# Every fourth key block weighed in f32, GpSimd without subtractions and sums, ScalarE's steps placed later: attention with a routed feed-forward layer on one core

## The reference

```python
xn = _layernorm(x)
# attention, 8 heads of 64, one key and one value head for all of them
xa = layer_norm(xn, norm_g)
q, (k, v) = xa @ Wq, split(xa @ Wkv)
q, k = l2norm(q * 16) * 4, l2norm(k) * 4
attn = softmax(einsum('bhid,bjd->bhij', q, k))          # 2048 x 2048 for each head
s = layer_norm(einsum('bhij,bjd->bhid', attn, v) @ Wout, out_norm_g)
# routed feed-forward layer: 8 experts, top 2, capacity 2560 rows each
wy = (gelu(xg @ w1 + b1) @ w2 + b2) * gating
g = silu(segment_sum(wy))
return x + s * g
```

## Time and profile before

| | |
|---|---|
| median of 3 runs | 3028.18 us |
| the profiled execution's own time | 3029.31 us |
| its span, first to last instruction | 3027.6 us |
| busy: PE, DVE, ACT, POOL | 2777.8, 2012.2, 1910.8, 1125.2 us |
| mean granted TensorE clock | 0.974 |

### The profile page before, as it was taken

One profiled execution on the slowest core, in us unless ns is written; L12 is line 12 of the kernel. 1 busy time (PEld: TensorE's weight loads), 2 busy tenths in 40 slices (PEclk: granted clock), 3 DMA queues, 4 the chain that ended last, 5 costly groups with the idle time before them and its releaser, 6 DMA issues.

```text
span 3027.6 us, 86214 instructions
## 1 busy us (share of the span) xinstructions
PE 2777.8 (92%) x38213; PEld 1847.3 (61%) x38277; DVE 2012.2 (66%) x2798; ACT 1910.8 (63%) x2435; POOL 1125.2 (37%) x707
## 2 busy tenths in 40 slices
PE   4999999988999989999999999999888889888896
PEld 3566666655666657666666666655555555555564
DVE  5777787789888733333333343378788888888775
ACT  6777767756766655565656565466666666666664
POOL 2444444414787400000000000055566656566454
PEclk8999999999999989999999999999999999999997
DMA  2213222003332011221121221101111111111101
GB/s 98 93 66 109 89 76 92 28 32 99 126 120 85 6 55 50 79 72 65 63 86 59 68 74 51 38 24 32 49 47 42 49 42 40 42 43 44 30 23 45
DMA packets 111013, 184.12 MB, mean 61 GB/s; under 512 B 12648, under 2 KB 78128, under 8 KB 110640
## 3 DMA queue, kind: packets, MB, share of 16 engines
q1 hardware_dynamic: 98352, 145.04, 14.6%
q0 software_dynamic: 12288, 33.57, 3.5%
HBM read 92.58 MB, written 85.98 MB: 59 GB/s over the span
## 4 chain that ended last, share of the span: by engine, by line
PE 64%; DVE 17%; ACT 9%; issue 7%; POOL 2%; DMA 1%; SPq 0%; ACTq 0%; DVEq 0%; POOLq 0%
PE pair L607 15%; PE bank L687 14%; PE pair L673 14%; DVE arena L1194 9%; ACT arena L843 6%; PE bank L637 5%; PE bank L628 4%; PE bank L626 4%; PE bank L588 2%; PE bank L546 2%; DVE o_rest L1129 1%; PE bank L657 1%; DVE q_n L1115 1%; POOL routed_rows L1271 1%; PE bank L576 1%
## 5 line engine op out<-in xcount | busy, mean ns | idle before, releaser
L1194 DVE TENSOR_TENSOR arena<-arena 128x1024 bf16<-128x1024 f32 (+1 forms) x817 | 1091.9, 1347 | 351.6 <-ACT arena L843 349.0
L843 ACT ACTIVATE arena<-pair 128x1024 f32<-128x1024 f32 (+1 forms) x1032 | 1017.2, 1015 | 319.4 <-PE pair L607 309.7
L607 PE MATMUL pair<-qT,kT 128*128 128x512 f16 (+1 forms) x4096 | 903.0, 388 | 136.7 <-ACT arena L843 133.6
L626 PE MATMUL bank<-vhl,arena 128*128 128x65 bf16 x8192 | 654.4, 194 | 4.0 <-DVE att L1187 4.0
L1313 POOL TENSOR_TENSOR arena<-arena 128x1024 bf16<-128x1024 f32 (+1 forms) x215 | 440.6, 2049 | 578.6 <-ACT arena L843 561.3
L628 PE MATMUL bank<-vhl,arena 128*128 128x64 bf16 x8192 | 655.0, 195 | 0.0
L626 PEld LDWEIGHTS bank<-vhl,arena 128*128 128x128 bf16 x8192 | 573.6, 100 | 56.3 <-DVE att L1187 4.4
L628 PEld LDWEIGHTS bank<-vhl,arena 128*128 128x128 bf16 x8192 | 555.3, 98 | 52.3 <-issue 1.9
L607 PEld LDWEIGHTS pair<-qT,kT 128*128 128x128 f16 (+1 forms) x4096 | 205.5, 96 | 598.8 <-issue 405.0
L1243 POOL TENSOR_TENSOR q_small<-q_small,minus_half 128x8 f32<-128x8 f32 x64 | 142.8, 2231 | 1015.8 <-DVE q_small L1111 1014.8
L637 PE MATMUL bank<-vhl,arena 128*128 128x65 bf16 x8192 | 421.2, 194 | 22.9 <-DVE arena L1194 17.1
(11 more groups left out here) (191 smaller groups left out, 2448.6 us busy)
## 6 DMA issues: line engine op xcount, KB each, us to landing
routed_rows<-h_f SPq DMA_DIRECT2D x80, 256.0 KB, 4.5
att<-routed_rows SPq DMA_DIRECT2D x40, 512.0 KB, 4.3
expert_rows<-att SPq DMA_DIRECT2D x40, 512.0 KB, 2.9
raw<-in_L_ffn_w SPq DMA_DIRECT2D x32, 512.0 KB
xn_rows<-s_hl SPq DMA_DIRECT2D x16, 512.0 KB, 2.9
xT_out<-xn_rows SPq DMA_DIRECT2D x64, 128.0 KB
w_lo<-in_L_attn_x SPq DMA_DIRECT2D x64, 128.0 KB
out<-w_lo SPq DMA_DIRECT2D x64, 128.0 KB, 2.0
```

The costliest lines, as they stand in the source:

```text
L607: t = nc.tensor.matmul(into, kT[g // BG % 2][rows, part, keys], qT[g % 2][rows, h, :], start=(turn == 0), stop=(turn == 1))
L626: nc.tensor.matmul(bank[:, at:at + DH + 1], p_top[:, s, cols, 1], V[:, kb, 0:DH + 1], start=(kb == 0 and qb == 0), stop=False, skip_group_ ...
L843: nc.scalar.activation(p_f32[:, n % NP, columns(n)], pairs[n % 2][:, columns(n)], ACT.Exp).then_inc(exped, 1)
L1194: nc.vector.tensor_tensor(p_lo[:, n % NP, c], p_f32[:, n % NP, c], p_top[:, n % NP, c, 1], ALU.subtract).then_inc(lowed, 1)
```

## The change

In steps with `n % 4 == 3` the key block is weighed with the f32 exponentials as stationary operand and a copy of the values in f32 (`v_f32`, with its column of ones) as moving operand: one matmul of 65 columns for each head and block of 128 queries in place of three. Such a step has no low weights. In the built program each f32 matmul is two weight loads and two matmuls. `low` is left on DVE alone, for three steps of four, in the scatter stretch too. The sum with x in `combine` goes from POOL to DVE. For later tiles some side steps are placed later by one or two slots.

```diff
-    on_pool = [n % 4 == 3 and not R_AT <= place["scores", n] < SCATTER_AT + 2 * NT for n in range(NSTEP)]
+    in_f32 = [n % GT == GT - 1 for n in range(NSTEP)]
+    low_to = np.cumsum([not wide for wide in in_f32]).tolist()
...
+        v_f32 = [sb(f"v_f32{i}", [P, BG, DH + 1], F32) for i in range(2)]
...
+                    if in_f32[n]:
+                        for qb in range(GT):
+                            cols = slice(i * BANK + qb * P, i * BANK + (qb + 1) * P)
+                            t = nc.tensor.matmul(bank[:, qb * (DH + 1):(qb + 1) * (DH + 1)], p_f32[:, s, cols],
+                                                 v_f32[b % 2][:, kb // GT, :], start=False, stop=(kb == KB - 1),
+                                                 skip_group_check=True)
+                        continue
...
-                pe.wait_ge(lowed, n + 1 - pool_to[n])
-                pe.wait_ge(lowed_pool, pool_to[n])
-                for i, g, h, kb in halves(n):
+                pe.wait_ge(lowed, low_to[n])
+                for i, g, h, kb in () if in_f32[n] else halves(n):
...
-                yield from clock.at(Q_AT[t_id] + 6)
+                yield from clock.at(Q_AT[t_id] + (6 if t_id < GT else 7))
...
-                yield from clock.at(C_AT[t_id] + 10)
+                yield from clock.at(C_AT[t_id] + 12)
                 act.wait_ge(f_both, i + 1)
...
+                nc.vector.memset(v_f32[b % 2][:, gi, DH:DH + 1], 1.0)
+                nc.vector.tensor_copy(v_f32[b % 2][:, gi, 0:DH], v_f[:, GT - 1, :])
...
-                yield from clock.at(Q_AT[t_id] + 7)
+                yield from clock.at(Q_AT[t_id] + (7 if t_id < GT else 9))
                 dve.wait_ge(q_hi, t_id + 1)
...
-                yield from clock.at(C_AT[t_id] + 9)
+                yield from clock.at(C_AT[t_id] + 10)
                 dve.wait_ge(f_first, i + 1)
...
-                yield from clock.at(C_AT[t_id] + 12)
+                yield from clock.at(C_AT[t_id] + 14)
                 dve.wait_ge(c_tanh, i + 1)
...
+                dve.wait_ge(c_times, i + 1)
+                dve.wait_ge(x_again_loaded[i % 2], 16 * (i // 2 + 1))
+                dve.wait_ge(out_stored[i % 2], 16 * (i // 2))
+                nc.vector.tensor_tensor(res[i % 2], w, x_again[i % 2], ALU.add).then_inc(c_added, 1)
...
-                    if a is not None and not on_pool[a]:
+                    if a is not None and not in_f32[a]:
                         low(a)
...
-                yield from clock.at(C_AT[t_id] + 14)
-                pool.wait_ge(c_times, i + 1)
-                pool.wait_ge(x_again_loaded[i % 2], 16 * (i // 2 + 1))
-                pool.wait_ge(out_stored[i % 2], 16 * (i // 2))
-                nc.gpsimd.tensor_tensor(res[i % 2], c_work[i % 2][:, D:2 * D], x_again[i % 2],
-                                        ALU.add).then_inc(c_added, 1)
-
-            def low(n):
-                pool.wait_ge(exped, n + 1)
-                pool.wait_ge(weighed, n - NP + 1)
-                c = columns(n)
-                nc.gpsimd.tensor_tensor(p_lo[:, n % NP, c], p_f32[:, n % NP, c], p_top[:, n % NP, c, 1],
-                                        ALU.subtract).then_inc(lowed_pool, 1)
...
-                yield from clock.at(C_AT[t_id] + 15)
+                yield from clock.at(C_AT[t_id] + 16)
                 sp.wait_ge(c_added, i + 1)
```

More of the change, by code:

```diff
@@ L199, in columns @@
         return slice(active[0] * BANK, (active[-1] + 1) * BANK)
-    on_pool = [n % 4 == 3 and not R_AT <= place["scores", n] < SCATTER_AT + 2 * NT for n in range(NSTEP)]
-    pool_to = np.cumsum(on_pool).tolist()
+    in_f32 = [n % GT == GT - 1 for n in range(NSTEP)]
+    low_to = np.cumsum([not wide for wide in in_f32]).tolist()
+    assert CUT % GT == 0 and BEHIND % GT == 0
     def last_step(hh):
@@ L361, in build_program @@
                              "q_hi", "q_lo", "q_turned", "qT_copied")]
-        scored, exped, lowed, lowed_pool, weighed = [sem(n) for n in (
-            "scored", "exped", "lowed", "lowed_pool", "weighed")]
+        scored, exped, lowed, weighed = [sem(n) for n in ("scored", "exped", "lowed", "weighed")]
         head_inv, divided = sem("head_inv"), sem("divided")
@@ L1301, in combine @@
                         bass.IndirectOffsetOnAxis(gather_from[k][:, t_id:t_id + 1], 0)).then_inc(y_gathered[i % 2], 16)
-                yield from clock.at(C_AT[t_id] + 14)
-                pool.wait_ge(c_times, i + 1)
-                pool.wait_ge(x_again_loaded[i % 2], 16 * (i // 2 + 1))
-                pool.wait_ge(out_stored[i % 2], 16 * (i // 2))
-                nc.gpsimd.tensor_tensor(res[i % 2], c_work[i % 2][:, D:2 * D], x_again[i % 2],
-                                        ALU.add).then_inc(c_added, 1)
-            def low(n):
-                pool.wait_ge(exped, n + 1)
-                pool.wait_ge(weighed, n - NP + 1)
-                c = columns(n)
-                nc.gpsimd.tensor_tensor(p_lo[:, n % NP, c], p_f32[:, n % NP, c], p_top[:, n % NP, c, 1],
-                                        ALU.subtract).then_inc(lowed_pool, 1)
             def main(kind, a, b):
-                if kind == "att" and a is not None and on_pool[a]:
-                    low(a)
+                pass
             clock.run(slots, main, [constants()] + [statistics(g) for g in reversed(range(NG))] + [route()] + [
```

## The result

The changed kernel takes 3064.3 us (median of 4 runs, 3063.76 to 3064.43) against 3028.5 us before (4 runs, 3024.03 to 3029.28): a ratio of 1.0121 with a 95% interval of 1.0103 to 1.0138. It is 36 us slower. The forecast was 73 us faster. The measured time lies inside the stated range of 2880 to 3115 us, but on the other side of the kernel before.

A forecast was written before the change was run, and what follows sets the result against it. PE was taken as the bound, its gaps ending a chain POOL, DVE, ACT. Terms -103 - 13 + 43 = -73 us on 3029.3 us gave 2956 us; range 2880 to 3115 us, the forecast's own 2905 to 3010.

The forecast's parts named there:

- the price of the f32 steps: PE's 256 f32 weighings: 0.058 us per load with its matmul, so +48 us, taken as +43 us.
- The bound from the loads: Upper bound for f32 steps: 0.077 us a record with loads beside matmuls, +127 us; one after the other, +363 us.
- the point of decision: An f32 record of 0.075 us on PE, above which the kernel is slower than before.
- the +248 us estimated from it: f32 term on PE by the skill page's 107 ns load: a step of 1.71 us, and the change would lose.
- Rival A: In PE's f32 steps the loads bind: 0.106 us a record, +245 us, 3158 us in all; chance 20%.
- The gaps: PE's waits in attention for late exponentials and low weights shrink: -103 and -13 us, together -116 us.
- a third of the late exponentials: Part of PE's 154 us of exponential waits left standing because ACT has own side work; two thirds taken, -103 us.
- half of the waits for low weights: PE's 26 us of waits for low weights halve as POOL's subtractions go: -13 us.
- All gaps gone: Lower end of the forecast's own range, 2905 to 3010 us: no gaps of PE left, put at -50 us.
- The cost at nothing for the sums on DVE: The 64 sums with x moved to DVE, 31 us of its time, taken as 0, upper bound +10 us.
- Rival B: PE's gaps stay: a later cast is late in its new place, PE's turn unmoved; 3048 us, chance 11%.

The follow-up runs named there:

- experiment 5: The changed kernel with 33 instead of 65 moving columns in each f32 matmul: 3060.5 us, one run.
- experiment 2: The changed kernel with no step in f32 and the side steps of q and `combine` back in their slots of before: 2920.3 us.
- experiment 9: The changed kernel with no step in f32, plus 215 useless POOL subtractions that read SBUF: 3178.8 us.
- experiment 10: The changed kernel with no step in f32, plus useless POOL memsets that only write, in place of subtractions: 2901.4 us.
- experiment 4: The kernel before with only the later slots, POOL still subtracting, its sum and the store one slot later: 3027.9 us, ratio 1.0005.
- experiment 1: The changed kernel with no step in f32, all 1032 steps in bf16 and all low weights made by DVE: 2900.3 us.
- experiment 8: The changed kernel with no step in f32 and the 64 sums with x back on POOL: 2901.3 us.

## Why the prediction was wrong

**The step that failed** is the price of the f32 steps, in the line that took 0.058 us "since the bf16 rows show loads wholly beside matmuls". It was sized by the stream. The load binds: 0.111 us from start to start, 0.108 on average over a step, so +253 us and not +48. The bf16 rows couldn't show this, because their loads are short enough to hide in 0.031 us; they show that loads lie beside matmuls, which is right for f32 too (at the upper clock 33 and 65 columns give the same 0.111 us), but not how long an f32 load is.

**The bound from the loads was too low.** The two f32 loads at the begin gave 0.155 us each, and half of that, 0.077 us, was taken for the upper clock. The halving was right: experiment 5 has 0.213 us at the lower clock and 0.111 at the upper. The 0.155 was not. It came from two matmuls behind an idle PE, with 8 rows of weights, and the starts there lie 0.129 and 0.180 us apart; that is no steady pace. Neither is their clock on record, since the clock's record begins at 29 us in that trace. Why they took less than 0.213 us stays open. With a true pace of 0.107 the bound would have stood above the point of decision, 0.075, with the stream wholly hidden.

**The load by the notes and by the runs.** The Trainium skill's figure (TensorE: Matmul & The Clock Gate, LDWEIGHTS (loading the stationary operand)), 128 / 1.2 = 107 ns for a load, is near the 0.111 to 0.112 us that the runs show at the upper clock, and the +248 us estimated from it agrees with the +253 measured. At the lower clock experiment 5 shows 0.213 us, twice the Trainium skill's figure, and there the measurement decides. By the runs 128 f32 weights take about 256 cycles at either clock (213 ns at 1.2 GHz, 107 and some 5 more at 2.4).

**Rival A was the case that came**, with its cause (the f32 loads bind) and by luck with its price: 0.106 us was the middle of two ends, of which one, load and stream in a row, is refuted by experiment 5. Its time, 3158 us, was 94 too high because the other term was too small.

**The stream's price was right**: about two cycles a column, 0.057 us for 65 columns, by the second starts of the groups (experiment 5).

**The gaps.** Forecast -116 us, measured 217 us less apart from the f32 term. The mechanism, POOL then DVE then ACT then PE, holds (experiments 2, 9 and 10), and so does its reading from one place. Three things were off. I let the moved slots share in the gain with POOL's leaving; by themselves they gain nothing (experiment 4) and with POOL quiet 20 us. I left a third of the late exponentials and half of the waits for low weights standing; nearly all went: 147 us of waits, 167 with the 0.16 us for each of the 130 waits that are gone. And I had no term for TensorE's clock. With fewer gaps the mean granted clock went from 0.974 to 0.990. PE was busy at the lower clock for 93 us before and for 19 us after (from 70 us on, without the last 45 us), and by the lengths of a weighing at the two clocks, 1.31 and 0.74 us, that is an estimated 32 us. That leaves 18 of the 217 us without a place.

From experiments 1 and 2 the parts are: POOL quiet and the sums moved -106, slots -20, f32 steps +164, which is 253 less 89 of gaps that they cover. Their sum is the difference of the kernels before and after by construction, and no check of its own.

**A slip in the range.** "All gaps gone" would have been 180 - 116 = 64 us below the forecast, not 50.

**The cost at nothing for the sums on DVE** was right within what experiment 8 can tell: 2901.3 and 2900.3 us.

**Rival B** named a wait that did come, at the turn of q, since `qhl`'s low part moved down and the turn did not. It didn't matter in the changed kernel (6.3 us), where PE is slow, but it costs 93.0 us in experiment 4 and 50.0 in experiment 1.

## What to carry to other kernels

Price a matmul by the longer of its load and its stream, each from a row of the same type, and from matmuls that follow each other without a gap. A type that never stands in the hot loop has no price there, and two records behind an idle engine give a wrong one, even when they are scaled rightly to the clock. Gaps of TensorE may cost twice, by their own length and by a lower clock: here an estimated 32 us beside 167. When a wait is the end of a chain, ask which engine is late, and expect the wait to move if only its place is changed. And look at two-input VectorE operations beside GpSimd ones that read: here the "free" help of POOL, 215 subtractions and 64 sums, cost 106 us, and a kernel that leaves it idle, stays in bf16 and turns q later takes 2877.7 us, 4.9% less than before.

## What the runs showed of the hardware

- An f32 matmul is two loads and two matmuls. One after the other, with 128 weights, they start 0.111 to 0.112 us apart at the upper clock whether 65 or 33 columns follow, and 0.213 us apart at the lower (33 columns). With 64 weights and 65 columns it is 0.058 to 0.059 us at the upper and 0.107 to 0.108 at the lower clock. A moving column costs about two cycles in each of the two matmuls (0.057 and 0.029 us for 65 and 33 columns).
- 128 bf16 weights load in at most 0.031 us (load and 65 columns together), so three bf16 products of split numbers, 0.093 us, are cheaper than one f32 product, 0.216 us, at 65 moving columns.
- GpSimd operations that read SBUF hold up VectorE operations with two inputs in SBUF until they are done: such a subtraction takes up to 4.57 us in place of 1.22. Memsets don't (longest 1.24 us), though a cast of k took up to 1.21 us in place of 0.43 behind them. The sums over q, with a single input, and operations with one input in PSUM were not stretched by the reads.
